# GpSimd's order in the heads' loop of a sparse graph-attention stack: weigh before the leaky add

## What is computed

```python
h = jnp.maximum(_layernorm(x, axis=-1), 0.0)
x = x + _L1_gnn_ref(h, adj, L1_gnn_Wh, ...)

def _gat_layer(h, mask, b):
    scores = jnp.einsum('...nd,...md->...nm', h, h)
    scores = jnp.where(mask, scores, NEG)
    attn = jax.nn.softmax(scores, axis=-1)
    return jnp.einsum('...nm,...md->...nd', attn, h) + b
# _L1_gnn_ref
h = jnp.einsum('bnc,hdc->bhnd', x, Wh)                    # 4 heads
out_h = _gat_layer(h, mask[None, None], bh[None, :, None, :])
cat = jnp.transpose(out_h, (0, 2, 1, 3)).reshape(B, N, H * D)
z = jax.nn.leaky_relu(cat, negative_slope=0.2)
h2 = jnp.einsum('bnk,dk->bnd', z, Wo)
out2 = _gat_layer(h2, mask[None], bo)                     # then leaky, LayerNorm
```

## Time and profile before

| | |
|---|---|
| median of 3 runs | 1940.18 us (1939.62 to 1941.21) |
| the profiled execution | 1944.53 us |
| its span, first to last instruction | 1942.6 us |
| busy over the span | VectorE 1337.7 us (69%), TensorE 1116.4 (57%), GpSimd 1032.4 (53%), ScalarE 778.5 (40%) |
| GpSimd: weigh, L680 (all stages) | 356 instructions, 361.9 us |
| GpSimd: leaky add, L687 | 64 instructions, 81.5 us |
| the heads' stage | about 480 to 1078 us |

### The profile page before, as it was taken

How to read it: one execution, slowest core, us unless ns; L and a number is a source line. 1 busy time by engine, 2 the same in 40 slices (tenths; PEclk the granted TensorE clock), 3 DMA queues, 4 the chain that set the end, 5 groups by cost and what they waited for, 6 DMA issues and landing times.

```text
span 1942.6 us, 13706 instructions
## 1 busy us (share of the span) xinstructions
PE 1116.4 (57%) x3112; PEld 559.7 (29%) x3112; DVE 1337.7 (69%) x1715; ACT 778.5 (40%) x2486; POOL 1032.4 (53%) x939
## 2 busy tenths in 40 slices
PE   0000445563898995999998433343437677646662
PEld 0000322221454443444444111111124334422220
DVE  7894748797899989668770376989768776424441
ACT  0400543442475663565566123343325554422210
POOL 0094357532677873867765555556447643237540
PEclk9999967776899997999999666676658878857776
DMA  9152465422221210011100323222035422046434
GB/s 339 65 86 87 154 206 157 123 82 87 59 77 38 87 54 22 22 44 38 44 12 11 119 81 103 71 65 76 17 106 149 142 77 76 17 133 194 142 114 104
DMA packets 101625, 178.79 MB, mean 92 GB/s; under 512 B 47552, under 2 KB 56032, under 8 KB 99232
## 3 DMA queue, kind: packets, MB, share of 16 engines
q0 software_dynamic: 30960, 102.92, 18.2%
q1 hardware_dynamic: 51216, 70.05, 11.0%
q10 hardware_dynamic: 19360, 4.87, 1.5%
HBM read 147.88 MB, written 34.12 MB: 94 GB/s over the span
## 4 chain that ended last, share of the span: by engine, by line
PE 39%; DVE 24%; issue 13%; POOL 12%; ACT 7%; DMA 4%; DVEq 0%; ACTq 0%; POOLq 0%; SPq 0%
PE PS L1220 19%; PE PS L1206 9%; ACT big L895 5%; POOL big L652 5%; POOL big L680 3%; DVE big L1680 3%; DVE big L1672 3%; PE PS L1168 2%; DVE big L1664 2%; PE PS L1243 2%; PE PS L1279 2%; PE PS L1231 2%; DVE big L1559 2%; DVE big L1478 1%; DVE big L1606 1%
## 5 line engine op out<-in xcount | busy, mean ns | idle before, releaser
L1220 PE MATMUL PS<-big,ident 128*128 128x512 f32 x1044 | 542.9, 675 | 298.8 <-POOL big L680 202.1
L895 ACT ACTIVATE big<-big 128x64 f32<-128x64 f32 x1632 | 404.3, 339 | 333.5 <-DVE big L1637 298.0
L680 POOL TENSOR_TENSOR big<-big 128x512 f32<-128x512 f32 x356 | 361.9, 1046 | 52.9 <-DVE big L1637 40.7
L1220 PEld LDWEIGHTS PS<-big,ident 128*128 128x128 f32 x1044 | 221.2, 217 | 579.2 <-issue 519.8
L1206 PE MATMUL PS<-big,ident 128*128 128x512 f32 x348 | 226.1, 816 | 167.4 <-ACT big L895 93.8
L1680 DVE TENSOR_REDUCE big<-big 128x32 f32<-128x2048 f32 (+4 forms) x126 | 297.7, 2362 | 4.3
L1672 DVE TENSOR_TENSOR big<-big,PS 128x2048 f32<-128x2048 f32 (+4 forms) x84 | 198.5, 2363 | 80.5 <-PE PS L1231 77.9
L652 POOL DMA_INDIRECT big<-tab,SI x142 | 175.0, 1233 | 132.9 <-PE PS L1206 63.8
L1206 PEld LDWEIGHTS PS<-big,ident 128*128 128x128 f32 x348 | 88.5, 265 | 303.8 <-issue 272.7
L652 POOL DMA_INDIRECT big<-h_rows,SI x142 | 138.5, 976 | 62.5 <-issue 27.4
L1168 PE MATMUL PS<-ident,big 128*128 128x128 f32 x640 | 102.4, 288 | 114.2 <-DMA big<-h_rows 52.2
(11 more groups left out here) (157 smaller groups left out, 1527.8 us busy)
## 6 DMA issues: line engine op xcount, KB each, us to landing
big<-in_adj SPq DMA_DIRECT2D x16, 1024.0 KB, 6.1
tab<-big SPq DMA_DIRECT2D x64, 132.0 KB, 1.8
big<-tab SPq DMA_DIRECT2D x32, 264.0 KB, 3.0
h_rows<-big SPq DMA_DIRECT2D x32, 256.0 KB, 2.0
big<-h_rows SPq DMA_DIRECT2D x32, 256.0 KB, 2.7
big<-in_x ACTq DMA_DIRECT2D x16, 256.0 KB, 5.0
big<-xs SPq DMA_DIRECT2D x4, 1024.0 KB, 9.8
h_table<-big SPq DMA_DIRECT2D x16, 256.0 KB, 2.0
```

Source lines behind the costliest of these rows:

```text
L680: ins = pool.tensor_tensor(bd(wbuf[:, i % NWB, j, :]), bd(rows[:, k + j, :]), over_d(S[:, h, k + j, :], B), ALU.mult)
L895: ins = act.activation(to, row, ACT.Copy, scale=S[:, h, k + j, b:b + 1])
L1220: mm = pe.matmul(to, ident[:, :], wbuf[:, i % NWB, k, :], start=(c == 0 and k == 0), stop=(c == len(parts) - 1 and k == n - f - 1))
```

## The change

In each step of GpSimd's loop over the heads, the weighing of job m-4 is moved ahead of the leaky add of job m-8. The gather stays last. No other engine's program changes, and GpSimd's instructions are the same ones.

```diff
                         for m in range(NT * HEADS + 10):
+                            if heads_job(m - 4):
+                                weigh(1, *heads_job(m - 4))
                             if 0 <= m - 8 < NT * HEADS:
                                 add_leaky(m - 8)
-                            if heads_job(m - 4):
-                                weigh(1, *heads_job(m - 4))
                             gather(1, m // HEADS + AHEAD, m % HEADS, HEADS)
```

## The result

The changed kernel took 1959.57 us in the median of 4 runs (1955.28 to 1963.1), the kernel before 1940.7 beside it (1939.62 to 1942.77). The ratio is 1.0092, with a 95% interval of 1.0079 to 1.0105, about 18 us slower (15 to 20). The forecast was 1957.1, in a range of 1948 to 1964.

A forecast was written before the change was run, and what follows sets the result against it. TensorE was taken to bound tiles 4 to 6 and the stage from tile 8 on, VectorE the stretches before and between; -2.0 + 3.3 + 0.9 + 10.7 + 4 = +16.9 on the median 1940.18 gave 1957.1 us, range 1948 to 1964.

The forecast's parts named there:

- The bound and the place: Heads' stage: GpSimd's idle time is not on the path; TensorE's lost time is, mainly at tile 8.
- Tile 8's waits, 10.7: Tile 8: L1243 waits 3.5, 4.3 and 4.3 us for adds behind last chunks, 1.4 given back; +10.7 us.
- The clock, 4: Tile 8: TensorE's clock falls after three gaps, six in seven costing 1.6 us each; +4 us.
- the rival without clock falls: Tile 8: the waits come but TensorE's clock doesn't fall; +12.9 us, 1953.1, chance 0.20.
- Tiles 4 to 6, 3.3: Tiles 4 to 6: L1243 waits for the add 1.75 us at job 13 and 1.5 at job 18; +3.3 us.
- VectorE's small adds, -2.0: End of tile 3: VectorE's first small add is free 2 us sooner, which shortens the path; -2.0 us.
- the rival in which VectorE gets in between GpSimd's instructions: End of tile 3: VectorE gets in after one GpSimd instruction, -4.4 instead of -2.0; 1954.7 us, chance 0.11.
- the 0.9: Tile 8's first divide: VectorE meets a run of GpSimd's instructions that it missed before; about +0.9 us.
- the missing wait at job 13: Tiles 4 to 6: TensorE's L1243 of job 13 was to wait 1.75 us for GpSimd's add.

The follow-up runs named there:

- e1: The kernel before with the new order only in the four steps that weigh tile 8 (13 slots, three chunks): 1955.06 us against 1939.86, ratio 1.0074.
- e6: The changed kernel with TensorE's multiply by W repeated to fill the three gaps at tile 8: 1952.24 us, ratio 1.0059 to the kernel before.
- e2: The kernel before with the new order only in the twelve steps that weigh tiles 4 to 6 (two chunks): 1943.98 us, ratio 1.0022.
- e3: The kernel before with the new order only in the steps that weigh tiles 0 to 3 (one chunk): 1941.5 us, ratio 1.0003.
- e5: The changed kernel, but in jobs of several chunks the leaky add stands directly ahead of the last chunk: 1939.88 us against 1940.35 for the kernel before.
- e4: The kernel before with the new order only in the steps that weigh tiles 7 and 9 to 15 (one chunk): 1940.18 us, ratio 1.0001.

## Why the prediction was right, and where it wasn't

**The bound and the place: right.** GpSimd's idle time was not on the path: its wait for ScalarE fell by 90 us, and nothing was gained. TensorE's time was: tile 8 alone (e1) costs 14.4 us.

**Tile 8's waits, 10.7: measured 11.05** (e6), or from the rows of after: L1243 to the next sum was 1.72 us for both jobs and is 804.11 - 798.89 = 5.22, so +3.50, as forecast; from L1279 to the turn behind L1243 it is 821.79 - 815.71 = 6.08 against 1.72, +4.36; the third +4.48. The wait of the queries for ScalarE is 0.69 instead of 2.10, -1.41. Sum 10.9. Every link of this walk had a row: a chunk of four, an add, a sum's length.

**The clock, 4: measured 4.52** by e6, and for this part of the sum the rival without clock falls (1953.1) is out. But its two factors were both off, and that 4 came out is luck. The forecast had 6 of 7 gaps slow at 1.6 us each. Of the three gaps the first (3.24) cost nothing, in the changed kernel and in e1 alike. The other two cost 2.3 each on average, and not alike: from one sum's start to the next, against e6, the stretch with the second gap is 2.05 us longer and the sum behind it 0.90 slow, 2.95 in all; the third gap is the remaining 1.7.

**Tiles 4 to 6, 3.3: the waits are there** (1.55 and 1.35 in e2; 4.3 us of time, 3.8 of the profiled stage). In the profile after it was otherwise. TensorE there:

```profile
593.01 5.40 PE L1220 MATMUL PS<-big,ident 128*128 128x512 f32 x8 [3.31 <-ACT big L956]
...
609.59 2.19 PE L1243 MATMUL PS<-big,WoB 128*128 128x512 f32 x4
...
662.38 1.13 PE L1243 MATMUL PS<-big,WoB 128*128 128x512 f32 x2 [1.35 <-POOL big L687]
```

The second wait is there (1.35), the first shrank to 0.31: L1243 of jobs 12 and 13 starts at 609.59 and takes 2.19 us instead of 1.88. The eight matmuls of add_up(15) had taken 5.40 us instead of 3.70. So TensorE started add_up(16) when it did before (124.26 us after the stage's start against 124.39), while GpSimd, fed by a VectorE that was 2 us early, ended add(13) at 133.5 us instead of the 135.2 of e2. Slow clock and wait took each other's place: at add_up(17) the profile is 0.17 us later than before, where -2.0 and +1.75 had been forecast.

**VectorE's small adds, -2.0: the step that failed.** The rows are as forecast:

```profile
545.65 1.04 DVE L1621 TENSOR_TENSOR big<-big,SI 128x128 f32<-128x128 f32 x1
...
547.14 3.99 DVE L1626 TENSOR_TENSOR big<-big,mx 128x128 f32<-128x128 f32 x1
551.74 2.29 DVE L1672 TENSOR_TENSOR big<-big,PS 128x2048 f32<-128x2048 f32 x1 [0.62 <-PE PS L1231]
```

3.03 + 3.98 became 1.04 + 3.99, 1.98 us less, so the rival in which VectorE gets in between GpSimd's instructions (-4.4) is out as well. What failed is the sentence that they "delay tile 4, ScalarE's exp(4) behind it and so add_up(15)": it took 2 us at VectorE to be 2 us at TensorE. e3 measured +0.6 for the part (-1.6 to +2.7). One piece goes to VectorE's wait for queries (0.62). The rest goes to TensorE's clock. In all four profiles with the new order there (the changed kernel, e3, e5, e6) add_up(15) started about 116.0 us after the stage's start instead of 117.6, but took 5.40 to 5.60 us instead of 3.70, and add_up(16) started at 124.3 to 124.6, as before. In the four with the old order it took 3.70 us in three and 6.45 in e4, which lost 1.9 us ahead of tile 8 by it. So the slow sum goes along with the early VectorE, 4 of 4 against 1 of 4, but why it does isn't shown. The term should have been about 0, with -2 as its lower bound. At tile 8's first divide the 0.9 was right: L1637 takes 1.23 instead of 0.36 us.

**The other miss: the tail.** Nothing was forecast behind tile 8, and the profile after gained 1.69 us there. TensorE at 1082, behind a gap of 2.91 us, then the same place in the kernel before:

```profile
1082.39 0.63 PE L1168 MATMUL PS<-ident,big 128*128 128x128 f32 x4 [2.91 <-ACT big L968]
1082.86 1.02 PE L1279 MATMUL PS<-big,WB 128*128 128x512 f32 x2
1083.72 1.88 PE L1243 MATMUL PS<-big,WoB 128*128 128x512 f32 x4
```

```profile
1066.49 0.63 PE L1168 MATMUL PS<-ident,big 128*128 128x128 f32 x4 [2.91 <-ACT big L968]
1066.96 1.74 PE L1279 MATMUL PS<-big,WB 128*128 128x512 f32 x2
1068.49 2.91 PE L1243 MATMUL PS<-big,WoB 128*128 128x512 f32 x4
```

The same gap, once with L1279 and L1243 at 1.02 and 1.88 us, once at 1.74 and 2.91. It goes with no order: e1, e2 and e4 had the quick kind, e3, e5 and e6 the slow one. So +16.97 against +16.9 for the profiled stage is partly luck: up to tile 8's end it came out 1.8 us above the forecast (0.9 in each of the first two stretches of the table; in tile 8 that is 0.2 of waits and 0.6 of clock), behind it 1.7 below. By the medians (+18.9) or the ratio (+17.9) the forecast was 1 to 2 us low. That is inside the interval, so it can't be put down to a term: the failed -2.0 points that way, but in the whole change the missing wait at job 13 made up for much of it.

## What to carry to other kernels

In a queue that runs in order, a short operation that another engine waits for must not stand behind one that has a wait of its own, above all one for a ring buffer that the waiting engine itself empties: walk that wait's release, step by step, before believing an idle share. The idle time that such a reorder is meant to use can be real and worth nothing; look which engine has no slack in that stretch, and price the longest gap that it gets there twice, once as time and once as clock. And where only part of a loop's iterations have the inner wait, as the jobs of two and three chunks here, the place inside the iteration matters (e5: no loss), not whether it is first or last.

## What the runs showed of the hardware

TensorE's clock, on one and the same gap, came out either way. After an idle 3.14 or 3.15 us ahead of tile 4's queries, these ran at full speed in two profiles (1.99 us) and at half speed in two (3.78); after the 2.91 us at the stage's end, four of eight profiles were slow. Three gaps of 3.24 to 4.22 us at tile 8 fell the same way in both profiles that had them: none, fall, fall. A fall cost between 1.3 us (the queries of tile 4 in the kernel before, 3.28 instead of 2.00) and 2.95 (behind tile 8's second gap), often some 1.7. e2 even had one behind a gap of only 2.10 us at tile 8 (queries 2.56 us, and 1.69 us on the tile), which cost nothing in the four other profiles with that gap. The Trainium skill ("TensorE: Matmul & The Clock Gate", What's actually happening) calls the gate's watcher free-running against the kernel, and these rows agree. Runs of the kernel before spread from 1937.1 to 1946.3 us, and such falls are a likely part of it, but no run was made to test it; the start of the heads' stage alone, 477.1 to 480.6 us in the eight profiles, differs by more than one fall. For a kernel with many gaps of 2 to 5 us this limits what one profile can say: a difference of 2 us in a stage needs the stage cut in stretches, as above, or many runs.

VectorE's small adds against a full GpSimd: the second one (L1626, both inputs in SBUF) took 3.98 to 4.00 us in all eight profiles, whether the run of GpSimd's three instructions beside it was add, slot, slot or slot, slot, add. The first one (L1621) took 3.03 us in the four profiles with the old order there and 1.03 or 1.04 in the four with the new, where only the add of the run was left. All sixteen ended within 0.2 us of the end of a run, none between two of its instructions. By the recorded starts the second one was even there first: in the kernel before it starts at 552.15, while a gather is being issued, and the run's first instruction at 552.71. The Trainium skill ("SBUF — State Buffer", Reading the diagram) gives the shared port to whoever starts first, for that instruction. If it is this port that VectorE waited for, which no run here tests, then a run of back-to-back instructions kept it to its end.
